# Attention in a one-core block kernel: high probabilities times the whole 129-column value row in one product for three of four query tiles, the low part added by VectorE

## The chip, the core and the metric

The kernel is written for one core of a Trainium2 chip. A core has TensorE (matrix products, with its own weight loads), VectorE, ScalarE and GpSimd, each with an instruction queue of its own that runs in order, and SyncE, which issues transfers. They share SBUF; products land in PSUM, eight banks of 512 fp32 columns. The metric is the device time of one execution, in microseconds, the median of several runs.

## What is computed

The input is `x`, 4 sequences of 1024 rows and 256 features. The reference adds to it, in turn, a linear recurrent block, a sparse feed-forward block, multi-head attention, and the feed-forward block again, each behind a layer norm. The change concerns attention:

```python
q = (x @ Wq.T).reshape(b, t, N_HEADS, HEAD_DIM)          # 8 heads of 64
kv_latent = x @ Wkv_down.T                               # 64 wide
k = (kv_latent @ Wk_up.T).reshape(b, t, N_HEADS, HEAD_DIM)
v = (kv_latent @ Wv_up.T).reshape(b, t, N_HEADS, HEAD_DIM)
scores = jnp.einsum('bqhd,bkhd->bhqk', q, k) * scale
attn = jax.nn.softmax(scores, axis=-1)
out = jnp.einsum('bhqk,bkhd->bqhd', attn, v)
return out.reshape(b, t, N_HEADS * HEAD_DIM) @ Wo.T
```

The kernel folds the up-projections into the query and output weights, so that all heads share the 64-wide latent as key and as value. To hold fp32 accuracy with fp16 products it splits the probabilities and the latent values into a high and a low fp16 part.

## The kernel before, in words

**Stages.** Recurrent block, first feed-forward block (the top-k rounds on VectorE), attention from about 500 to 1150 us, second feed-forward block. The order of work on each engine is written out by hand; engines meet through semaphores only.

**Items.** Attention is a loop over 64 items `W`: 4 batches, 8 heads, 2 chunks of 512 queries. In an item the key tile `kt` runs from 0 to 7 (128 keys each). TensorE issues, for each `kt`: `scores(W, kt)` (L2021 and L2023, two 512-column products), then `max_scores(W + 2, kt)` (L2009, one 512-column product on strided queries, used to find a row maximum two items ahead), then, at `kt` 3, 4, 6 and 7, one query tile `j` of `weighted(W - 1, j)`, and at some places "slot work": query and key projections, turns and the output projection of neighbouring batches (L1929 to L1967). Batch 0 has hardly any slot work.

**The other engines.** ScalarE takes the exponential of each score tile (L1154) and copies it to fp16 as the high part (L1162); one probability tile buffer `pr` serves all items, `pr_hi` and `pr_lo` are double. The low part, probability minus high part, is subtracted by GpSimd for key tiles 1, 2, 3, 5, 6, 7 (L830) and by VectorE for 0 and 4 (L1628). VectorE also reduces each `max_scores` product (L1602) in the order of tiles; three PSUM banks serve these, so `max_scores` number n waits for reduce n - 3. At the end of an item VectorE does `largest` (L1610) and then `normalise(W - 1)` (L1619 reciprocal, L1621 multiply by it, written to `o_sb`). In some items it adds the output projection to `x` (L1591) and takes layer-norm statistics (L1284, L1293).

**The product that is changed.** `lat` holds for each key a row of 1 + 64 + 64 fp16 numbers: a one, the high part of the latent value and its low part. For each query tile `j` and key tile, `weighted` issues three products into a 65-column strip of bank 5: high probabilities times [one, high value] (L2038, 65 columns), high probabilities times low value into the same columns 1 to 64 (L2039, 64 columns), low probabilities times [one, high value] (L2040, 65 columns). Column 0 becomes the sum of the probabilities. Ahead of query tile 0 of an item it waits for the latent values, for `a_O` (the previous item was normalised), and for the last low parts of VectorE and GpSimd. The last item has a function of its own, `weighted_last`, which writes to four banks and is not changed.

`out_turn` (L1960) transposes `o_sb` for the output projection of a batch and waits on `a_O` for all items of that batch, the last of which is normalised at the end of the first item of the next batch.

Of the kernel before, what the change touches and what calls it, by code (L numbers as in the profile page):

```python
# [9 lines left out]
ALU = mybir.AluOpType  # L10
# [7 lines left out]
CH = 512  # L18
NCH = ROWS // CH
TPC = CH // P  # L20
# [4 lines left out]
HD = 64  # L25
# [22 lines left out]
def hybrid_block_kernel(nc, x_in, W_in, b_in, params_log, W_mid, b_mid, w1_w, w1_b, w2_w, w2_b,  # L48
# [4 lines left out]
    with ctx:  # L53
# [3 lines left out]
        def sem(name):  # L57
            return ctx.enter_context(nc.semaphore(name))
# [49 lines left out]
        def carve(shape, dt=F32, parts=P):  # L108
            n = 1
            for s in shape:  # L110
                n *= s
            words = n if dt == F32 else (n + 1) // 2
            a = arena[0:parts, room[0]:room[0] + words]
            room[0] += words
            assert room[0] <= ARENA, room[0]
            if dt != F32:
                a = a.bitcast(dt)
            if len(shape) == 2:
                a = a.rearrange("p (a b) -> p a b", a=shape[0])
            if len(shape) == 3:  # L120
                a = a.rearrange("p (a b c) -> p a b c", a=shape[0], b=shape[1])
            return a
# [66 lines left out]
        pr_hi = [carve([TIME // P, CH], F16) for _ in range(2)]  # L189
        pr_lo = [carve([TIME // P, CH], F16) for _ in range(2)]  # L190
# [8 lines left out]
        lat = [carve([TIME // P, 1 + 2 * HD], F16) for _ in range(2)]  # L199
        mx = [carve([TPC]) for _ in range(2)]  # L200
        mx_half = [carve([TPC, 2]) for _ in range(2)]
        mx_row = [carve([TPC], F16) for _ in range(2)]
        rden = carve([TPC])
        o_sb = [xcT[:, :].rearrange("p (t d) -> p t d", t=TIME // P), carve([TIME // P, NH * HD])]
        staged = [o_sb[1].rearrange("p t d -> p (t d)")[:, i * 2 * CH // 2:(i + 1) * 2 * CH // 2].bitcast(F16)
                  .rearrange("p (h t) -> p h t", h=2) for i in range(2 * GROUPS)]
# [22 lines left out]
        psum = ctx.enter_context(nc.psum_tensor("banks", [P, 8, 512], F32))  # L229
        ps = [psum[:, i, :] for i in range(8)]  # L230
# [109 lines left out]
        a_lP = sem("a_exp_low_pool")  # L340
        a_ops = sem("a_out_psum")
        a_O = sem("a_out")
        a_ft = sem("a_oT_psum")
        a_fe = sem("a_oT")
        a_fm = sem("a_final_psum")
# [11 lines left out]
        KT = TIME // P  # L357
        MX = TPC
        L_STEPS = 10
        ALL = BATCH * ITEMS  # L360
# [61 lines left out]
        def low_done(W, kt):  # L422

            if W == ALL - 1:
                return ((W * len(LOW_DVE) + LAST_DVE.index(kt)) if kt in LAST_DVE else
                        (W * len(LOW_POOL) + LAST_POOL.index(kt))) + 1
            if kt in LOW_DVE:
                return W * len(LOW_DVE) + LOW_DVE.index(kt) + 1
            return W * len(LOW_POOL) + LOW_POOL.index(kt) + 1
# [15 lines left out]
        def place(W):  # L445

            B, w = W // ITEMS, W % ITEMS
            hh, c = w // 2, w % 2
            return B, hh, c, hh % Q_RING
# [24 lines left out]
        def wait_from(engine, sem_, value):  # L474

            if value > 0:
                engine.wait_ge(sem_, value)
# [759 lines left out]
        def _(dve):  # L1237
# [374 lines left out]
            def normalise(W):  # L1612

                B, hh, c, slot = place(W)
                o = ps[5][:, 0:TPC * (HD + 1)].rearrange("p (t d) -> p t d", t=TPC)
                if W == ALL - 1:
                    o = psum[:, 0:TPC, 0:HD + 1]
                dve.wait_ge(a_ops, W + 1)
                nc.vector.reciprocal(rden, o[:, :, 0]).then_inc(a_O, 1)  # L1619
                dve.wait_ge(a_O, W * 2 + 1)  # L1620
                nc.vector.tensor_tensor(o_sb[B % 2][:, c * TPC:c * TPC + TPC, hh * HD:hh * HD + HD],  # L1621
                                        o[:, :, 1:1 + HD],
                                        rden.unsqueeze(2).to_broadcast([P, TPC, HD]), ALU.mult).then_inc(a_O, 1)
# [20 lines left out]
            for W in range(ALL):  # L1644
                B, w = W // ITEMS, W % ITEMS
                for kt in range(KT):
                    if W + 2 < ALL:
                        largest_of(W + 2, kt)
                    if kt in (LAST_DVE if W == ALL - 1 else LOW_DVE):
                        low(W, kt)  # L1650
                    if kt == 5 and w in STATS_AT and AHEAD <= B + 1 < BATCH:
                        chunk = 2 * B + 2 + STATS_AT[w]
                        dve.wait_ge(f_x, chunk * TPC + TPC + CREDIT["f_x"])
                        stats_of("ffn", chunk)
                    if kt in (3, 7):
                        what, n, part = beside(W, kt // 7)
                        bank = BESIDE[kt // 7]
                        if what == "query":
                            query_low(n, part, bank)
                        if what == "out_final":  # L1660
                            final(n, bank)
                        if what == "keys":
                            keys_low(n, part, bank)
                if W + 2 < ALL:
                    largest(W + 2)
                if W:
                    normalise(W - 1)
            final((BATCH - 1) * FINALS - 1, 4)
            normalise(ALL - 1)
            for j in range(FINALS):  # L1670
                final((BATCH - 1) * FINALS + j, 6 + j % 2)
# [20 lines left out]
        def _(pe):  # L1692
            mm = nc.tensor.matmul
# [105 lines left out]
            def bank_for(n):  # L1799

                if n >= 2:
                    pe.wait_ge(s_ev0, n - 1)
                return ps[4 + n % 2]

            for k in range(KB2):
                o = bank_for(k)
                nc.tensor.transpose(o[:, 0:P], lin_n[:, k, :], ident[:, :]).then_inc(s_pe0, 1)
            for k in range(KB2):
                o = bank_for(2 + k)
                nc.tensor.transpose(o[:, 0:HD], wd_n[:, k * P:k * P + P], ident[0:HD, 0:HD]).then_inc(s_pe0, 1)  # L1810
            for a in range(NH // 2):
                o = bank_for(4 + a)
                for k in range(KB2):
                    last = nc.tensor.transpose(o[:, k * P:k * P + P], wo_n[:, k, a * P:a * P + P], ident[:, :])
                last.then_inc(s_pe0, 1)
            lru_u(1, 1, (0, 1))
            for a in range(NH // 2):
                o = bank_for(8 + a)
                pe.wait_ge(s_ev0, 5 + a)
                for r in (0, HD):  # L1820
                    last = mm(o[r:r + HD, 0:D], wv_n[r:r + HD, a, :], woT[r:r + HD, a, :], start=True, stop=True)
                last.then_inc(s_pe0, 1)
            for k in range(KB2):
                for odd in range(2):
                    o = bank_for(12 + 2 * k + odd)
                    for a in range(NH // 2):
                        rows = slice(HD * odd, HD * odd + HD)
                        last = mm(o[:, a * HD:a * HD + HD], wq_n[rows, a, k * P:k * P + P], wk_n[rows, a, :],
                                  start=True, stop=True)
# [196 lines left out]
            def weighted(W, j):  # L2026


                B, c = W // ITEMS, W % 2
                if j == 0:  # L2030
                    pe.wait_ge(a_l, B * 2 + 2)
                    wait_from(pe, a_O, W * 2)
                    pe.wait_ge(a_lD, low_done(W, LOW_DVE[-1]))
                    pe.wait_ge(a_lP, low_done(W, LOW_POOL[-1]))
                o = ps[5][:, j * (HD + 1):(j + 1) * (HD + 1)]
                js = slice(j * P, j * P + P)
                for kt in range(KT):
                    mm(o, pr_hi[c][:, kt, js], lat[B % 2][:, kt, 0:1 + HD], start=kt == 0, stop=False)  # L2038
                    mm(o[:, 1:1 + HD], pr_hi[c][:, kt, js], lat[B % 2][:, kt, 1 + HD:], start=False, stop=False)  # L2039
                    last = mm(o, pr_lo[c][:, kt, js], lat[B % 2][:, kt, 0:1 + HD], start=False, stop=kt == KT - 1)  # L2040
                if j == TPC - 1:
                    last.then_inc(a_ops, 1)

# [70 lines left out]
            for W in range(ALL):  # L2114
                for kt in range(KT):
                    scores(W, kt)
                    if W + 2 < ALL:
                        max_scores(W + 2, kt)
                    if kt in WEIGHTED_AT and W:
                        weighted(W - 1, WEIGHTED_AT[kt])  # L2120
                    if kt < 2:
                        slot_work(W, 0, kt)
                    if kt in (2, 5):
                        slot_work(W, 1, kt // 5)
# [45 lines left out]
```

## Time and profile before

| | |
|---|---|
| median of 3 runs | 1370.94 us (1370.88 to 1372.45) |
| profiled execution | 1372.7 us, its span 1371.0 us |
| TensorE products | 1221.7 us busy, 89% |
| VectorE | 1146.8 us, 84% |
| ScalarE | 1052.5 us, 77% |
| GpSimd | 960.3 us, 70% |
| L2038, L2039, L2040 | 2016 products each, 193, 195 and 192 ns shown |

The span is the time from the first to the last instruction of one profiled execution. "Busy" counts an instruction from its start to its shown end; neighbouring products overlap on TensorE, so its pace is read from the distances between starts. In rows of the timeline the columns are start in us, length in us, engine, line, operation, output and input by name, shape, how many merged into the row, and in brackets how long the engine had been idle and for whom it waited.

### The profile page before, as it was taken

How to read it: one execution, taken by the hardware profiler on the slowest of the kernel's cores; microseconds unless marked ns; L12 is line 12 of the kernel's file. 1: busy time of each engine (PE TensorE's matmuls, PEld its weight loads, DVE VectorE, ACT ScalarE, POOL GpSimd, SP SyncE). 2: the span in 40 equal slices, each digit the busy share in tenths (PEclk: the TensorE clock that was granted, in tenths of full speed). 3: DMA queues.
4: the chain of work that ended last, by engine and by line, in shares of the span. 5: the costliest groups of instructions: out<-in, count | busy, mean ns of one | idle time of the engine just before them, and what ended most of it. 6: DMA issues, size and time to landing. Idle time of an engine off the chain costs nothing.

```text
span 1371.0 us, 30692 instructions
## 1 busy us (share of the span) xinstructions
PE 1221.7 (89%) x10214; PEld 748.0 (55%) x10214; DVE 1146.8 (84%) x3145; ACT 1052.5 (77%) x2346; POOL 960.3 (70%) x1095
## 2 busy tenths in 40 slices
PE   4999999866888889999999999999999999777776
PEld 2455554434545446665666666676666666344443
DVE  7999998599998878888777788877877854799998
ACT  3432333787899859999989989999999986787776
POOL 4457644478787767777776778777777773488887
PEclk9999999998999989999999999999999999799998
DMA  6200000000002100000000000000000000000000
GB/s 173 79 1 1 1 0 0 1 1 1 24 32 78 39 1 25 25 25 25 25 14 13 2 2 2 2 2 2 2 2 2 2 2 1 1 32 17 31 16 32
DMA packets 35529, 25.32 MB, mean 18 GB/s; under 512 B 16358, under 2 KB 32044, under 8 KB 35372
## 3 DMA queue, kind: packets, MB, share of 16 engines
q1 hardware_dynamic: 35372, 23.36, 6.0%
q8 instruction: 82, 1.34, 0.4%
q14 instruction: 75, 0.61, 0.1%
HBM read 14.89 MB, written 8.39 MB: 17 GB/s over the span
## 4 chain that ended last, share of the span: by engine, by line
PE 44%; ACT 13%; issue 11%; DVE 9%; POOL 4%; DVEq 0%; ACTq 0%; POOLq 0%
PE banks L2021 7%; PE banks L2023 6%; PE banks L2009 6%; PE banks L1967 4%; DVE arena L1526 4%; PE banks L2038 4%; PE banks L2039 4%; PE banks L2040 3%; ACT arena L1154 3%; DVE arena L1521 3%; ACT arena L1162 2%; PE banks L1943 2%; PE banks L2080 2%; ACT arena L1016 1%; DVE arena L1602 1%
## 5 line engine op out<-in xcount | busy, mean ns | idle before, releaser
L830 POOL TENSOR_TENSOR arena<-arena 128x512 f16<-128x512 f32 x383 | 437.6, 1162 | 151.0 <-ACT arena L1162 147.0
L1154 ACT ACTIVATE arena<-banks 128x512 f32<-128x512 f32 x512 | 303.0, 599 | 45.4 <-PE banks L2023 40.9
L1602 DVE TENSOR_REDUCE arena<-banks 128x1 f32<-128x512 f32 x512 | 325.5, 679 | 7.8 <-PE banks L2009 5.5
L1162 ACT ACTIVATE arena<-arena 128x512 f16<-128x512 f32 x512 | 316.1, 632 | 0.0
L2038 PE MATMUL banks<-arena 128*128 128x65 f16 x2016 | 211.3, 193 | 0.9
L1521 DVE MAX8 arena<-arena 128x8 f32<-128x256 f32 x512 | 190.1, 413 | 25.7 <-issue 13.9
L2039 PE MATMUL banks<-arena 128*128 128x64 f16 x2016 | 211.4, 195 | 0.0
L2040 PE MATMUL banks<-arena 128*128 128x65 f16 x2016 | 210.5, 192 | 0.0
L1628 DVE TENSOR_TENSOR arena<-arena 128x512 f16<-128x512 f32 x129 | 106.8, 828 | 123.4 <-ACT arena L1162 123.3
L1526 DVE MATCH_REPLACE8 arena<-arena 128x256 f32<-128x256 f32 x512 | 205.8, 409 | 1.7 <-issue 1.2
L2038 PEld LDWEIGHTS banks<-arena 128*128 128x128 f16 x2016 | 187.9, 96 | 31.8 <-issue 9.9
L2039 PEld LDWEIGHTS banks<-arena 128*128 128x128 f16 x2016 | 187.3, 97 | 27.1
L2021 PE MATMUL banks<-arena 128*128 128x512 f16 x512 | 194.1, 379 | 8.4 <-ACT arena L1154 6.7
L2009 PE MATMUL banks<-arena 128*128 128x512 f16 x512 | 195.1, 383 | 4.3 <-DVE arena L1602 4.0
L2023 PE MATMUL banks<-arena 128*128 128x512 f16 x512 | 193.8, 378 | 0.0
L2040 PEld LDWEIGHTS banks<-arena 128*128 128x128 f16 x2016 | 187.3, 99 | 0.0
L1890 PE MATMUL banks<-fW,arena 128*128 128x256 f32 x256 | 81.9, 448 | 31.8 <-ACT arena L1042 31.8
L2009 PEld LDWEIGHTS banks<-arena 128*128 128x128 f16 x512 | 57.9, 113 | 74.9 <-DVE arena L1602 16.2
L1877 PE MATMUL banks<-fW,arena 128*128 128x256 f32 x256 | 77.2, 431 | 0.0
L2021 PEld LDWEIGHTS banks<-arena 128*128 128x128 f16 x512 | 50.3, 98 | 48.9 <-ACT arena L1154 31.3
L1890 PEld LDWEIGHTS banks<-fW,arena 128*128 128x128 f32 x256 | 47.5, 206 | 51.9 <-ACT arena L1042 47.5
L1869 PE MATMUL banks<-lin,xcT 128*128 128x512 f32 x128 | 70.0, 629 | 0.4 <-ACT xcT L1046 0.4
(230 smaller groups left out, 2543.1 us busy)
## 6 DMA issues: line engine op xcount, KB each, us to landing
arena<-q_store SPq DMA_DIRECT2D x48, 128.0 KB, 2.7
x<-in_L_attn_a_x SPq DMA_DIRECT2D x8, 512.0 KB, 3.9
q_store<-arena SPq DMA_DIRECT2D x32, 128.0 KB, 1.8
out<-x SPq DMA_DIRECT2D x7, 512.0 KB, 2.9
arena<-arena SPq DMA_DIRECT2D x64, 1.0 KB, 1.9
arena<-in_L_attn_a_W_in SPq DMA_DIRECT2D x1, 768.0 KB, 5.6
arena<-in_L_attn_a_W_mid SPq DMA_DIRECT2D x1, 512.0 KB, 7.0
arena<-in_L_attn_a_w_w SPq DMA_DIRECT2D x2, 256.0 KB, 7.5
```

The lines of the kernel that those rows point to most:

```text
L830: nc.gpsimd.tensor_tensor(pr_lo[c][:, kt, :], pr[:, kt, :], pr_hi[c][:, kt, :], ALU.subtract).then_inc(a_lP, 1)
L1154: nc.scalar.activation(pr[:, kt, :], ps[6 + kt % 2][:, :], ACT.Exp, scale=SM_SCALE).then_inc(a_P, 1)
L1162: nc.scalar.activation(pr_hi[c][:, kt, :], pr[:, kt, :], ACT.Copy).then_inc(a_hi, 1)
L1521: nc.vector.max(m8[p][:, i, r, :], src).then_inc(f_k[i], 1)
L1526: nc.vector.match_replace(wk[p][:, i, r % 2, :], m8[p][:, i, r, :], src, TAKEN).then_inc(f_k[i], 1)
L1602: nc.vector.tensor_reduce(mx_half[c][:, i // 2, i % 2:i % 2 + 1], ps[n % MAX_BANKS][:, :], X, ALU.max).then_inc(a_mx, 1)
L2009: mm(ps[n % MAX_BANKS][:, :], every[:, j, :], kA[B % 2][:, half * CH:half * CH + CH], start=True, stop=True).then_inc(a_mps, 1)
L2021: mm(o[:, :], kA[B % 2][:, kt * P:kt * P + P], qA[:, slot, c * CH:c * CH + CH], start=True, stop=False)
L2023: mm(o[:, :], kB[B % 2][:, kt * P:kt * P + P], qB[:, slot, c * CH:c * CH + CH], start=False, stop=True).then_inc(a_sps, 1)
L2038: mm(o, pr_hi[c][:, kt, js], lat[B % 2][:, kt, 0:1 + HD], start=kt == 0, stop=False)
L2039: mm(o[:, 1:1 + HD], pr_hi[c][:, kt, js], lat[B % 2][:, kt, 1 + HD:], start=False, stop=False)
L2040: last = mm(o, pr_lo[c][:, kt, js], lat[B % 2][:, kt, 0:1 + HD], start=False, stop=kt == KT - 1)
```

## The change

For query tiles 0 to 2 the two products with the high probabilities become one of 129 columns, into a strip of 129 columns of bank 5; the third product, with the low probabilities, still goes to the first 65 of them. The strip of tile 3 starts at column 387 and only has 125 columns left, so that tile keeps its three products. `normalise` now takes the strips 129 apart. For every item but the last it first copies the low strips of three tiles (3 x 64 columns) to a new SBUF tile `o_low`, takes the reciprocal, adds `o_low` onto columns 1 to 64 of the three tiles in PSUM, and then multiplies as before. The semaphore `a_O_low` orders copy, add and multiply on VectorE.

```diff
@@ -201,6 +201,7 @@
+        o_low = carve([TPC - 1, HD])
@@ -340,6 +341,7 @@
+        a_O_low = sem("a_out_low_part")
@@ -1612,11 +1614,19 @@
             def normalise(W):
 
                 B, hh, c, slot = place(W)
-                o = ps[5][:, 0:TPC * (HD + 1)].rearrange("p (t d) -> p t d", t=TPC)
+                o = psum[:, :, :].rearrange("p b c -> p (b c)")[:, 5 * CH:5 * CH + TPC * (1 + 2 * HD)]
+                o = o.rearrange("p (t d) -> p t d", t=TPC)
+                dve.wait_ge(a_ops, W + 1)
                 if W == ALL - 1:
                     o = psum[:, 0:TPC, 0:HD + 1]
-                dve.wait_ge(a_ops, W + 1)
+                else:
+                    nc.vector.tensor_copy(o_low, o[:, 0:TPC - 1, 1 + HD:]).then_inc(a_O_low, 1)
                 nc.vector.reciprocal(rden, o[:, :, 0]).then_inc(a_O, 1)
+                if W < ALL - 1:
+                    dve.wait_ge(a_O_low, W * 2 + 1)
+                    nc.vector.tensor_tensor(o[:, 0:TPC - 1, 1:1 + HD], o[:, 0:TPC - 1, 1:1 + HD], o_low,
+                                            ALU.add).then_inc(a_O_low, 1)
+                    dve.wait_ge(a_O_low, W * 2 + 2)
                 dve.wait_ge(a_O, W * 2 + 1)
@@ -2032,12 +2042,16 @@
-                o = ps[5][:, j * (HD + 1):(j + 1) * (HD + 1)]
+                o = ps[5][:, j * (1 + 2 * HD):min(CH, (j + 1) * (1 + 2 * HD))]
                 js = slice(j * P, j * P + P)
                 for kt in range(KT):
-                    mm(o, pr_hi[c][:, kt, js], lat[B % 2][:, kt, 0:1 + HD], start=kt == 0, stop=False)
-                    mm(o[:, 1:1 + HD], pr_hi[c][:, kt, js], lat[B % 2][:, kt, 1 + HD:], start=False, stop=False)
-                    last = mm(o, pr_lo[c][:, kt, js], lat[B % 2][:, kt, 0:1 + HD], start=False, stop=kt == KT - 1)
+                    if j < TPC - 1:
+                        mm(o, pr_hi[c][:, kt, js], lat[B % 2][:, kt, :], start=kt == 0, stop=False)
+                    else:
+                        mm(o[:, 0:1 + HD], pr_hi[c][:, kt, js], lat[B % 2][:, kt, 0:1 + HD], start=kt == 0, stop=False)
+                        mm(o[:, 1:1 + HD], pr_hi[c][:, kt, js], lat[B % 2][:, kt, 1 + HD:], start=False, stop=False)
+                    last = mm(o[:, 0:1 + HD], pr_lo[c][:, kt, js], lat[B % 2][:, kt, 0:1 + HD], start=False,
+                              stop=kt == KT - 1)
```

## Rows read from the trace of the kernel before

**Rows 1.** The page: busy us, share of the span, instructions of each engine.
```profile
PE 1221.7 (89%) x10214; PEld 748.0 (55%) x10214; DVE 1146.8 (84%) x3145; ACT 1052.5 (77%) x2346; POOL 960.3 (70%) x1095
```

**Rows 2.** Reciprocals (L1619) in three stretches: ns min/median/max, first and last start.
```profile
L1619 DVE RECIPROCAL arena<-banks x11: 171/172/175, 514.1 to 599.5; 128x4 f32<-128x4 f32 x11
...
L1619 DVE RECIPROCAL arena<-banks x44: 163/172/183, 633.8 to 1083.6; 128x4 f32<-128x4 f32 x44
...
L1619 DVE RECIPROCAL arena<-banks x3: 171/172/172, 1083.6 to 1100.7; 128x4 f32<-128x4 f32 x3
```

**Rows 3.** Windows: length, busy us of PE, PEld, DVE, ACT, POOL, clock, DMA share, GB/s.
```profile
514.00:599.50 85.50, 84.67 (x1202) 52.59 (x1201) 70.88 (x132) 82.99 (x172) 67.95 (x61) 1.00 0.09 25
633.00:1083.60 450.60, 441.42 (x5557) 294.49 (x5556) 355.59 (x693) 413.54 (x824) 338.44 (x328) 1.00 0.03 6
```

**Rows 4.** Chain of work by line, 514 to 599.5 us and 640 to 1083 us.
```profile
by line: PE banks L2021 22.5%; PE banks L2023 20.2%; PE banks L2009 20.2%; PE banks L2038 13.1%; PE banks L2039 11.7%; PE banks L2040 11.4%; issue 1.0%
...
by line: PE banks L2021 12.9%; PE banks L2023 12.6%; PE banks L2009 12.2%; PE banks L1967 8.2%; PE banks L2039 7.0%; PE banks L2040 6.8%; ACT arena L1154 6.8%; PE banks L2038 6.7%; PE banks L1943 5.6%; issue 5.0%; ACT arena L1162 4.5%; DVE 
```

**Rows 5.** Timeline of TensorE, batch 0: one burst of weighted and its neighbours.
```profile
558.39 0.38 PE L2009 MATMUL banks<-arena 128*128 128x512 f16 x1
558.82 0.19 PE L2038 MATMUL banks<-arena 128*128 128x65 f16 x1
...
559.56 0.38 PE L2021 MATMUL banks<-arena 128*128 128x512 f16 x1
...
559.99 0.38 PE L2009 MATMUL banks<-arena 128*128 128x512 f16 x1
```

**Rows 6.** Timeline of GpSimd and ScalarE, batch 0.
```profile
555.29 3.38 POOL L830 TENSOR_TENSOR arena<-arena 128x512 f16<-128x512 f32 x3 [1.01 <-ACT arena L1162]
...
561.63 0.60 ACT L1154 ACTIVATE arena<-banks 128x512 f32<-128x512 f32 x1 [0.25 <-PE banks L2023]
...
563.83 3.38 POOL L830 TENSOR_TENSOR arena<-arena 128x512 f16<-128x512 f32 x3 [1.01 <-ACT arena L1162]
```

**Rows 7.** Timeline of TensorE: 128-column fp16 products at 958.92 us.
```profile
958.92 0.28 PE L1951 MATMUL banks<-ident,arena 128*128 128x128 f16 x2
959.03 0.38 PE L2021 MATMUL banks<-arena 128*128 128x512 f16 x1
```

**Rows 8.** Timeline of VectorE, batch 0, from one item's normalise on.
```profile
556.77 0.16 DVE L1610 TENSOR_REDUCE arena<-arena 128x4 f32<-128x8 f32 x1
556.84 0.17 DVE L1619 RECIPROCAL arena<-banks 128x4 f32<-128x4 f32 x1
557.05 0.42 DVE L1621 TENSOR_TENSOR xcT<-banks,arena 128x256 f32<-128x256 f32 x1
557.39 0.68 DVE L1602 TENSOR_REDUCE arena<-banks 128x1 f32<-128x512 f32 x1
558.30 0.93 DVE L1628 TENSOR_TENSOR arena<-arena 128x512 f16<-128x512 f32 x1 [0.24 <-ACT arena L1162]
559.15 2.47 DVE L1602 TENSOR_REDUCE arena<-banks 128x1 f32<-128x512 f32 x4
562.78 0.69 DVE L1628 TENSOR_TENSOR arena<-arena 128x512 f16<-128x512 f32 x1 [1.15 <-ACT arena L1162]
563.39 0.68 DVE L1602 TENSOR_REDUCE arena<-banks 128x1 f32<-128x512 f32 x1
```

**Rows 9.** Timeline of VectorE and TensorE at 676 us.
```profile
675.89 0.68 DVE L1602 TENSOR_REDUCE arena<-banks 128x1 f32<-128x512 f32 x1
...
676.63 0.41 PE L2009 MATMUL banks<-arena 128*128 128x512 f16 x1
```

**Rows 10.** Waits, 640 to 1083 us: us in total, times, longest.
```profile
DVE arena L1628 <- ACT arena L1162: 83.9, 76, 1.8
```

**Rows 11.** Who waited for L1621, and two such places in TensorE's timeline.
```profile
  PE banks L1960: 3.5, 3
...
812.30 0.63 PE L1960 MATMUL banks<-ident,arena 128*128 128x128 f32 x4 [1.67 <-DVE arena L1621]
812.76 0.38 PE L2021 MATMUL banks<-arena 128*128 128x512 f16 x1
...
1132.46 0.74 PE L1960 MATMUL banks<-ident,arena 128*128 128x128 f32 x5 [1.48 <-DVE arena L1621]
```

## The prediction

> **What bounds the kernel now.** I read the share of busy time first [rows 1]: TensorE 89% and VectorE 84% of the span, so neither can be dismissed, and the average says nothing about the stage that is changed. The change lies wholly in the attention stage, where 64 items run one after another; I next read their pace and the windows. Items of batch 0 follow each other at 8.54 us (eleven from 514.1 to 599.5), the three from 1083.6 to 1100.7 too; those between, with query, turn and output work beside them, at 10.5 us (44 from 633.8 to 1083.6) [rows 2]. In both stretches TensorE's modelled busy time is 98 to 99%, ScalarE's 92 to 97%, VectorE's 79 to 83% [rows 3]. The chain of work points to TensorE [rows 4]: the three product lines of `weighted` (L2038 to L2040) hold 36% of it in batch 0 and 20.5% from 640 to 1083 us, where other engines stand between.
>
> In batch 0 that share misleads, and I follow one period. `weighted` starts at 558.82 [rows 5] because GpSimd's last subtraction is done (three from 555.29, 3.38 us, so at 558.67 [rows 6]). After it come two bursts and two pairs of score products, then exponential 5 on ScalarE (561.63, 0.25 us idle for TensorE), then GpSimd's next three subtractions from 563.83 [rows 6], done at 567.21, and `weighted` again at about 567.35. This loop, 8.53 us, holds only two of the four bursts.
>
> **The products.** In 63 items (the last has code of its own) three of four query tiles lose one 64-column product for each of 8 key tiles: 63 x 3 x 8 = 1512 products and their weight loads go, and as many products grow from 65 to 129 columns. A burst of 24 products runs from 558.82 to 559.56 [rows 5]: 0.74 us, or 92 ns for each group of three; products overlap, so I count starts and not the 190 ns that one is shown to take. The trace has no 129-column product. Two fp16 products of 128 columns start at 958.92 and the next work at 959.03 [rows 7]: 55 ns each; one more column, by the 0.215 us of 512 columns (two between 559.56 and 559.99, rows left out between them), makes about 56. With one low product at 29 to 33 ns (a third of 92 is 31) a group is 85 to 89 ns. I take 85.5, since a long product leaves the next weight load time: 6.5 ns saved a group, 0.05 us a burst, 0.155 us an item. Bounds: 3 and 7 ns.
>
> The Trainium skill (TensorE: Matmul & The Clock Gate, section Back-to-back issue gap) speaks against the change: a stream of weight loads with 128-column matmuls sustains some 81 ns for each, not 56. This trace does not agree so far, with 55 ns [rows 7], though in a run of only two. By that figure a group would take about 110 ns instead of 92.
>
> **What VectorE gets.** `normalise` gains a copy of 3 x 64 values out of PSUM and an add of that size into PSUM, with two waits for the engine's own results. The trace has neither. The multiply of 256 values is shown as 0.42 us and gives way after 0.34 (557.05 to 557.39); reduces of 512 follow each other every 0.60 (four in 2.47 us, the last shown as 0.68) [rows 8]. That is 1.0 ns a value, so 192 values occupy 0.27 us and are shown as 0.35. An operation that needs the one before starts 0.04 us after its shown end (556.84 + 0.17, then 557.05). So: copy at 0, reciprocal at 0.27, add at 0.39, multiply at 0.78; before, the multiply came 0.21 after the reciprocal. Added: 0.57 us an item. Bounds: 0.45 if the copy runs twice as fast, 0.75 if the write into PSUM and the waits cost 0.1 each more.
>
> Queued behind it on VectorE are the largest-of reduce 0 (L1602), the subtraction of key tile 0 (L1628) and reduces 1 to 4. TensorE's `max_scores` i+3 must have reduce i, and stands in its queue ahead of `weighted`. TensorE's own wait on `a_O` comes 2 us later and stays covered, except at output turns (below).
>
> *The 17 plain items.* VectorE idles 0.24 us before the subtraction at 558.30. Reduce 1 ends at 559.15 + 0.69 = 559.84 and max_scores 4 starts at 559.99 [rows 5, 8]; where it truly waits, the gap is 0.05 (675.89 + 0.68 to 676.63 [rows 9]), so 0.10 is slack. New loop: subtraction 4 (562.78), reduces 5 to 7, `normalise`, reduce 0, subtraction 0, reduce 1, max_scores 4, a burst, exponential 5, subtraction 4. Its length: 8.53 + 0.57 - 0.24 - 0.10 - 0.05 = 8.71. Against that, the subtraction at 558.30 holds the engine 0.85 us, beside GpSimd's that runs until 558.67 [rows 6], while the one at 562.78 holds it 0.61 [rows 8]. Started a third of a microsecond later it hardly meets that work: up to 0.24 less, 8.47. The old loop would give 8.53 - 0.10 = 8.43. I take 8.56, nearer to the short ends because both effects are seen in rows: +0.03 x 17 = +0.5 us. Ends 8.43 and 8.71: -1.7 to +3.1.
>
> *The 43 others.* There VectorE's subtractions wait for ScalarE 76 times, 1.10 us in the mean [rows 10], nearly every one of two an item; the added 0.57 vanishes in the first of them. The gain is what the chain holds: 20.5% of 443 us is 91, three quarters of it in changed bursts, x 6.5/92 = -4.8 us. At 3 ns it is -2.2; if every burst counted, 43 x 0.155 = -6.7.
>
> *Where `normalise` is itself waited for.* TensorE's turn of the output (L1960) waits for the multiply three times, 3.5 us in all [rows 11], because VectorE was occupied by statistics; each costs the full 0.57: +1.7 us. Two of them are at 812.30 and, behind the last item, 1132.46. At 675.89 a reduce behind `normalise` is awaited without slack [rows 9]: +0.5. For a few items with little slack I add 0.2, an estimate.
>
> **Sum.** +0.5 - 4.8 + 1.7 + 0.7 = -1.9 us. The profiled execution has a span of 1371.0 and a time of 1372.7; the difference goes to the median of the runs, 1370.94: 1369.0.
>
> **The rivals.**
> 1. *TensorE's gain goes through almost whole.* For: TensorE is busy 98% in the window of the 43. -1.7 from the plain items, -6.7, +2.4: 1364.9. Against: ScalarE has 92% there, so some of the gain must end in a wait for it.
> 2. *VectorE takes over the period of the plain items* (slower). Place: the wait of max_scores 4 for reduce 1. It decides once the addition exceeds 0.39 us while the subtraction keeps its 0.85. At 0.75 the period is 8.89: +6.1 for 17 items, output turns +2.3, the other places +1.0, products -4.8: +4.6, 1375.5. For: VectorE's order is fixed and only 1.4 us of such an item is idle [rows 8]. Against: the shrinking overlap with GpSimd.
> 3. *The wide product does not run at its columns' pace.* Priced half way between the fp16 pace of 55 ns and that of fp32 products of 128 columns (four in 0.46 us, 812.30 to 812.76 [rows 11], 115 ns): 85, a group 115, 23 ns more, 0.55 us an item. 43 x 0.55 x two thirds on the chain is +15.8, two bursts of 0.18 in 17 items +6.3, VectorE +2.4: 1395.4. Rows 7 speak against it.
>
> The skill's page named above gives about the product pace of rival 3.
>
> **How the numbers follow.** The forecast, 1367 to 1371.5, has 45%, rival 1 25%, rival 2 25%, rival 3 5%. The range of 8 in 10 is 1364.0 to 1376.0: it takes in rivals 1 and 2 and leaves rival 3 out. A measurement of this kernel can tell 0.2%, 2.7 us, from no change. Faster than 1368.2 are rival 1 and a third of the forecast's case, 0.39; slower than 1373.7 are 18 in 25 of rival 2 and rival 3, 0.23; within, 0.38.
>
> **What would show it.** Starts inside a changed burst: 56 and 29 ns alternating, the burst 0.685 us; if the second is 33, the gain halves. Reciprocals of batch 0 8.56 us apart: 8.43 means that VectorE never binds, 8.7 or more that it does, with a gap on TensorE ahead of L2009. The multiply 0.78 us after the copy's start. The three waits for the output turn longer by 0.57 each. I should be wrong most easily on the chain's share in the 43 items, since a faster TensorE meets ScalarE sooner.

## The result, and the profile of the changed kernel

| | kernel before | changed kernel |
|---|---|---|
| median | 1371.24 us (20 runs, 1368.09 to 1374.29) | 1374.11 us (20 runs, 1371.87 to 1378.33) |
| ratio | | 1.002, 95% interval 1.0012 to 1.0029 |
| profiled execution | 1372.7 us, span 1371.0 | 1374.12 us, span 1372.4 |

The change costs 2.9 us, 0.2%, where 1.9 us less had been forecast. The page shows both parts of the change: TensorE has 1512 products fewer and 9 us less to do, VectorE 31 us more [rows 1].

```profile
PE 1212.9 (88%) x8702; PEld 739.0 (54%) x8702; DVE 1177.6 (86%) x3271; ACT 1052.7 (77%) x2346; POOL 958.8 (70%) x1095
```

In the windows that answer to [rows 3], batch 0 and the items after it, TensorE is busy 97% where it was 98 to 99, and VectorE 84 to 85% where it was 79 to 83.

```profile
514.00:599.80 85.80, 83.64 (x960) 51.70 (x959) 72.99 (x150) 83.27 (x170) 67.53 (x61) 1.00 0.09 25
635.10:1085.10 450.00, 437.16 (x4519) 290.08 (x4520) 378.96 (x775) 411.86 (x820) 335.78 (x326) 1.00 0.03 6
```

The timeline of TensorE in a plain item, which answers to [rows 5], shows the new burst: from 557.85 to 558.55, 0.70 us where it was 0.74. A product of 129 columns gives way after 0.05 to 0.06 us, the low product behind it after 0.03. Ahead of the burst `max_scores` 3 starts at 557.48, and it has been waiting for VectorE's reduce.

```profile
557.48 0.41 PE L2019 MATMUL banks<-arena 128*128 128x512 f16 x1 [0.17 <-DVE arena L1604]
557.85 0.22 PE L2049 MATMUL banks<-arena 128*128 128x129 f16 x1
557.90 0.19 PE L2053 MATMUL banks<-arena 128*128 128x65 f16 x1
557.93 0.22 PE L2049 MATMUL banks<-arena 128*128 128x129 f16 x1
557.99 0.19 PE L2053 MATMUL banks<-arena 128*128 128x65 f16 x1
...
558.55 0.38 PE L2031 MATMUL banks<-arena 128*128 128x512 f16 x1
```

In this item the burst starts 0.37 us behind the product that had waited. That is not typical: from 514 to 618 us the distance is 0.24 to 0.25 us in 11 of 13 items and 0.30 in one. The item after it shows the common case, with GpSimd's three subtractions ahead, which end at 566.16:

```profile
562.78 3.38 POOL L832 TENSOR_TENSOR arena<-arena 128x512 f16<-128x512 f32 x3 [1.19 <-ACT arena L1164]
...
566.20 0.41 PE L2019 MATMUL banks<-arena 128*128 128x512 f16 x1 [0.17 <-DVE arena L1604]
566.44 0.22 PE L2049 MATMUL banks<-arena 128*128 128x129 f16 x1
```

VectorE's timeline of the first of these two items answers to [rows 8]. From the copy at 555.62 to the multiply at 556.40 are 0.78 us. The subtraction at 557.34 has no idle time in front of it any more, and it holds the engine 0.60 us and not 0.85.

```profile
555.54 0.16 DVE L1612 TENSOR_REDUCE arena<-arena 128x4 f32<-128x8 f32 x1
555.62 0.35 DVE L1623 COPY arena<-banks 128x192 f32<-128x192 f32 x1
555.88 0.17 DVE L1624 RECIPROCAL arena<-banks 128x4 f32<-128x4 f32 x1
556.00 0.37 DVE L1627 TENSOR_TENSOR banks<-banks,arena 128x192 f32<-128x192 f32 x1
556.40 0.42 DVE L1631 TENSOR_TENSOR xcT<-banks,arena 128x256 f32<-128x256 f32 x1
556.74 0.68 DVE L1604 TENSOR_REDUCE arena<-banks 128x1 f32<-128x512 f32 x1
557.34 0.68 DVE L1638 TENSOR_TENSOR arena<-arena 128x512 f16<-128x512 f32 x1
557.94 2.48 DVE L1604 TENSOR_REDUCE arena<-banks 128x1 f32<-128x512 f32 x4
561.73 0.69 DVE L1638 TENSOR_TENSOR arena<-arena 128x512 f16<-128x512 f32 x1 [1.31 <-ACT arena L1164]
```

**Where the time went.** Whole spans are a poor measure here: the work ahead of attention, which the change does not touch, took 0.5 to 4.1 us less in the profiles of the experiments than in that of the kernel before. So I take the starts of ScalarE's exponential of key tile 0 in each item. The distance to the next one is that item's time, and the tail runs from item 63's to the last turn of the output (L1960). The plain items are 2 to 16, 59 and 60. The table gives the differences in us against the profile of before; its last three columns are the two runs that do one part alone (below) and their sum:

| | before | changed | VectorE's part alone | products alone | the two added |
|---|---|---|---|---|---|
| items 0 and 1 | 16.81 | -0.11 | +0.01 | -0.09 | -0.08 |
| 17 plain items | 145.36 | +1.01 | +1.95 | -1.10 | +0.85 |
| 40 later items | 415.04 | -2.92 | +0.07 | -2.93 | -2.86 |
| item 17 (output turn) | 10.76 | +0.93 | +0.94 | -0.03 | +0.91 |
| item 20 | 9.48 | +0.51 | +0.58 | -0.07 | +0.51 |
| item 33 (output turn) | 12.79 | +2.04 | +0.58 | +0.12 | +0.70 |
| item 49 | 11.32 | +0.27 | +0.18 | +0.01 | +0.19 |
| tail (output turns) | 28.12 | +1.74 | +2.10 | -0.06 | +2.04 |
| sum | | +3.47 | +6.41 | -4.15 | +2.26 |

The products bring 4.2 us, most of it in the later items, where VectorE's extra work costs nothing. Of what the changed kernel loses, 1.0 us lies in the plain items and 5.5 in four items and the tail, places where VectorE is late with layer-norm statistics. The two parts added explain the changed kernel to within 0.3 us in each line but that of item 33, where 1.3 us are unexplained by them.

**The half clock.** The windows of the changed kernel show what is in item 33 and in the tail. The column behind the five engines is the granted clock.

```profile
810.00:812.80 2.80, 0.45 (x4) 0.22 (x3) 2.54 (x12) 1.59 (x3) 2.38 (x4) 1.00 0.00 0
812.80:816.00 3.20, 3.20 (x24) 2.31 (x23) 3.20 (x6) 1.49 (x3) 0.32 (x1) 0.50 0.01 3
1133.60:1137.20 3.60, 3.60 (x13) 2.85 (x11) 0.00 (x0) 1.19 (x2) 0.58 (x2) 0.53 0.00 0
```

The kernel before kept the full clock behind the same two waits:

```profile
812.20:816.00 3.80, 3.70 (x61) 2.78 (x61) 3.77 (x7) 2.47 (x6) 1.89 (x2) 1.00 0.00 0
1132.40:1136.00 3.60, 3.20 (x20) 2.77 (x21) 0.13 (x1) 1.08 (x2) 1.02 (x2) 1.00 0.00 0
```

TensorE's timeline of the changed kernel, beside [rows 11]: it had waited 2.35 us and 2.06 us for `normalise`, where it had been 1.67 and 1.48. Behind the first wait its 512-column products start 0.42 to 0.43 us apart (813.33, 813.75, 814.18) and not 0.215: 1.2 GHz in place of 2.4.

```profile
812.61 0.93 PE L1970 MATMUL banks<-ident,arena 128*128 128x128 f32 x4 [2.35 <-DVE arena L1631]
813.33 0.63 PE L2031 MATMUL banks<-arena 128*128 128x512 f16 x1
813.75 0.64 PE L2033 MATMUL banks<-arena 128*128 128x512 f16 x1
814.18 0.63 PE L2019 MATMUL banks<-arena 128*128 128x512 f16 x1
...
1133.21 1.54 PE L1970 MATMUL banks<-ident,arena 128*128 128x128 f32 x8 [2.06 <-DVE arena L1631]
1134.67 3.14 PE L1977 MATMUL banks<-voB,arena 128*128 128x256 f32 x8
1137.65 0.60 PE L1970 MATMUL banks<-ident,arena 128*128 128x128 f32 x4
```

### The profile page after: what moved, and what is told of

It reads as the page before. It is cut to its first block, busy times and chain, and to the rows that moved or that the text cites. A ratio compares the mean times of both kernels' runs of the same rounds, so it can differ in the third digit from the quotient of the medians.

```text
span 1372.4 us, 27857 instructions
## 1 busy us (share of the span) xinstructions
PE 1212.9 (88%) x8702; PEld 739.0 (54%) x8702; DVE 1177.6 (86%) x3271; ACT 1052.7 (77%) x2346; POOL 958.8 (70%) x1095
## 4 chain that ended last, share of the span: by engine, by line
PE 33%; ACT 19%; issue 12%; DVE 10%; POOL 6%; DVEq 0%; DMA 0%; SPq 0%; POOLq 0%; ACTq 0%
ACT arena L1156 6%; ACT arena L1164 5%; PE banks L2031 4%; PE banks L2033 4%; PE banks L2019 4%; PE banks L1977 4%; DVE arena L1528 4%; POOL arena L832 3%; PE banks L2049 3%; DVE arena L1523 3%; PE banks L2053 2%; PE banks L1953 2%; PE banks L2094 2%; ACT arena L1018 1%; DVE arena L1604 1%
## 5 line engine op out<-in xcount | busy, mean ns | idle before, releaser
L2053 PE MATMUL banks<-arena 128*128 128x65 f16 x2016 | 205.7, 193 | 0.0
L2053 PEld LDWEIGHTS banks<-arena 128*128 128x128 f16 x2016 | 181.4, 98 | 19.7 <-issue 0.3
L1638 DVE TENSOR_TENSOR arena<-arena 128x512 f16<-128x512 f32 x129 | 103.0, 798 | 94.7 <-ACT arena L1164 93.0
L2049 PE MATMUL banks<-arena 128*128 128x129 f16 x1512 | 158.1, 221 | 0.1
L2049 PEld LDWEIGHTS banks<-arena 128*128 128x128 f16 x1512 | 136.7, 97 | 19.6 <-issue 2.2
L1900 PE MATMUL banks<-fW,arena 128*128 128x256 f32 x256 | 80.3, 441 | 32.0 <-ACT arena L1044 32.0
L2019 PEld LDWEIGHTS banks<-arena 128*128 128x128 f16 x512 | 57.9, 113 | 83.7 <-DVE arena L1604 27.1
L2031 PEld LDWEIGHTS banks<-arena 128*128 128x128 f16 x512 | 50.2, 98 | 49.9 <-ACT arena L1156 29.6
L1887 PE MATMUL banks<-fW,arena 128*128 128x256 f32 x256 | 72.8, 411 | 0.0
L768 POOL TENSOR_TENSOR arena<-arena 128x256 f32<-128x256 f32 x63 | 45.8, 727 | 32.0 <-ACT arena L1039 27.8
L1025 ACT ACTIVATE arena<-arena 128x256 f32<-128x256 f32 x128 | 57.9, 503 | 12.7 <-DVE arena L1528 12.7
## 6 DMA issues: line engine op xcount, KB each, us to landing
x<-in_L_attn_a_x SPq DMA_DIRECT2D x8, 512.0 KB, 3.8
out<-x SPq DMA_DIRECT2D x7, 512.0 KB, 2.9
arena<-in_L_attn_a_W_mid SPq DMA_DIRECT2D x1, 512.0 KB, 7.5
```

The lines of the kernel that those rows point to most:

```text
L1900: last = mm(ps[6][:, 0:D], sxT[p][:, k, :], fW[:, k, :], start=k == 0, stop=k == KB2 - 1)
L2019: mm(ps[n % MAX_BANKS][:, :], every[:, j, :], kA[B % 2][:, half * CH:half * CH + CH], start=True, stop=True).then_inc(a_mps, 1)
L2031: mm(o[:, :], kA[B % 2][:, kt * P:kt * P + P], qA[:, slot, c * CH:c * CH + CH], start=True, stop=False)
L2049: mm(o, pr_hi[c][:, kt, js], lat[B % 2][:, kt, :], start=kt == 0, stop=False)
L2053: last = mm(o[:, 0:1 + HD], pr_lo[c][:, kt, js], lat[B % 2][:, kt, 0:1 + HD], start=False, stop=kt == KT - 1)
```

## The experiments

My theory was: TensorE's saving is real and partly hidden; VectorE's 0.57 us costs in plain items and at the output turns; and two longer waits of TensorE lower its clock. The rivals: the wide product saves nothing, VectorE's work is hidden, or the extra time in item 33 and the tail is VectorE's delay itself.

### One part alone

VectorE's part alone:

```diff
-                        mm(o, pr_hi[c][:, kt, js], lat[B % 2][:, kt, :], start=kt == 0, stop=False)
+                        mm(o[:, 0:1 + HD], pr_hi[c][:, kt, js], lat[B % 2][:, kt, 0:1 + HD], start=kt == 0, stop=False)
+                        mm(o[:, 1 + HD:], pr_hi[c][:, kt, js], lat[B % 2][:, kt, 1 + HD:], start=False, stop=False)
```

> VectorE's part alone: the strips lie 129 apart and VectorE copies and adds as in the change, but tiles 0 to 2 keep two short products for the high probabilities (65 and 64 columns). Theory (VectorE's 0.57 us costs by itself, at output turns with a half-clock stretch behind them; TensorE's saving gives a part back): items of batch 0 at 8.68 us, the time 6 to 9 us over the kernel before. Rival (VectorE's work is hidden, the loss is the wide product's): within 1 us of before.

Measured: 1377.69 us against 1370.94 of the kernel before on the same chip, ratio 1.0048 (1.0035 to 1.0061), +6.7 us. Plain items take 8.66 us (598.1 less 511.5, by 10).

```profile
L1624 DVE RECIPROCAL arena<-banks x11: 170/172/173, 511.5 to 598.1; 128x4 f32<-128x4 f32 x11
```

The products alone. The low part of the values is left out for three of four query tiles, so this kernel's results are not complete (lines between the cut ones are left out here):

```diff
-                    nc.vector.tensor_copy(o_low, o[:, 0:TPC - 1, 1 + HD:]).then_inc(a_O_low, 1)
...
-                    nc.vector.tensor_tensor(o[:, 0:TPC - 1, 1:1 + HD], o[:, 0:TPC - 1, 1:1 + HD], o_low,
-                                            ALU.add).then_inc(a_O_low, 1)
```

> TensorE's part alone: wide products as in the change, but no copy and no add in normalise, so the low part of the values is left out for three of four query tiles. Theory: items of batch 0 at 8.45 us, the 43 items behind them a few hundredths to 0.2 us shorter each, in all 4 us below the kernel before. Rival (the wide product saves nothing that counts): within 1 us of before.

Measured: 1367.40 us against 1370.94, ratio 0.9972 (0.996 to 0.9984), -3.5 us; plain items 8.48 us. Both rivals fall. The products do pay, VectorE's part is dearer, and the two results, +6.7 and -3.5, give +3.2, about the 2.9 of the whole.

```profile
L1622 DVE RECIPROCAL arena<-banks x11: 171/172/175, 512.8 to 597.6; 128x4 f32<-128x4 f32 x11
```

### TensorE kept busy in its two long waits

TensorE gets eight products of 512 columns, whose results nobody reads, ahead of the output turn of item 33 and of the first one behind item 63 (there into bank 7):

```diff
                 if what == "out_turn" and half == 0:
+                    if W == 2 * ITEMS + 1:
+                        kept_busy(bank, 8)
...
+                    if j == 0:
+                        kept_busy(7, 8)
                     out_turn(J, j % 2)
```

> The changed kernel, with eight products of 512 columns of no use (1.7 us) put into TensorE's two long waits, ahead of the output turn in item 33 and of the one behind item 63. Theory (the waits, 2.7 and 2.2 us, let the granted clock fall to half for the next 3.5 us): granted clock 1.00 behind both waits, item 33 shorter by 1.4 us, the tail by 1.2, the time 2.6 us below the changed kernel. Rival (the extra 2 us there are VectorE's delay itself): same as the changed kernel or a little longer.

The 2.7 and 2.2 us of this expectation run from the start of the product before the wait to the start of the one behind it; the idle time in the rows above is 2.35 and 2.06. Measured: 1370.06 us against 1370.94, ratio 0.9992 (0.9982 to 1.0003). Item 33 is +0.62 above before, not +2.04; the tail +0.44, not +1.74; every other line of the table stays within 0.25 us of the changed kernel's. So the half clock cost 1.4 and 1.3 us. VectorE's delay at the two places is then about 0.6 and 0.4 us. Windows behind the waits:

```profile
811.00:815.00 4.00, 3.47 (x32) 2.04 (x31) 3.74 (x14) 2.03 (x5) 1.85 (x3) 1.00 0.01 2
1133.00:1137.00 4.00, 3.66 (x20) 3.21 (x20) 0.42 (x1) 1.35 (x3) 0.11 (x1) 1.00 0.01 4
```

The same products in the kernel before:

> The same useless products in the kernel before, whose waits are 2.0 and 1.7 us and where the profiled execution kept the full clock. Theory: no change, within 0.5 us, unless other executions of the kernel before lose the clock there too. Rival: any gain would mean that they do.

Measured: 1370.78 us against 1370.94, ratio 0.9996 (0.9988 to 1.0005). The kernel before gains nothing from them, so its waits do not cost it the clock. The rival "it is VectorE's delay itself" falls.

To see whether the half clock was an accident of one execution, the changed kernel unaltered:

> The changed kernel once more, unaltered, beside the three below. Theory (the half-clock stretches belong to the change in most executions): item 33 and the tail again 2.0 and 1.7 us above the kernel before, the time 2.5 to 3.5 us above it. Rival (one execution's accident): item 33 only 0.6 above, no stretch at half clock.

Measured: 1373.24 us against 1371.42, ratio 1.0016 (1.0007 to 1.0024). Item 33 +2.05, tail +1.83, and the granted clock behind the waits is 0.54 both times:

```profile
812.80:816.00 3.20, 3.20 (x24) 2.21 (x24) 3.20 (x6) 1.65 (x3) 0.47 (x1) 0.54 0.01 3
1133.60:1137.20 3.60, 3.51 (x13) 2.69 (x12) 0.00 (x0) 1.19 (x2) 0.58 (x2) 0.54 0.00 0
```

VectorE's part alone shows the other side: it lost the clock in the tail (+2.10) but not in item 33 (+0.58), though TensorE had waited 2.24 us there. So the length of the wait does not settle it alone. The timed runs give only the total, so how often it is lost in each place stays open.

```profile
813.25 0.63 PE L1970 MATMUL banks<-ident,arena 128*128 128x128 f32 x4 [2.24 <-DVE arena L1631]
...
813.30:817.00 3.70, 3.70 (x61) 2.70 (x61) 3.67 (x7) 2.52 (x6) 1.16 (x2) 1.00 0.01 2
```

### VectorE's addition doubled

The second copy and add work on the low strips, which nobody reads afterwards (the first wait's new number and the last wait are left out):

```diff
+                    nc.vector.tensor_copy(o_low2, o[:, 0:TPC - 1, 1 + HD:]).then_inc(a_O_low, 1)
+                    dve.wait_ge(a_O_low, W * 4 + 3)
+                    nc.vector.tensor_tensor(o[:, 0:TPC - 1, 1 + HD:], o[:, 0:TPC - 1, 1 + HD:], o_low2,
+                                            ALU.add).then_inc(a_O_low, 1)
```

> The changed kernel with a second copy and a second add of the same shape in normalise, on the low strips that nobody reads afterwards: VectorE gets another 0.65 to 0.8 us an item. Theory (the 0.57 of the change hides in VectorE's wait of 1.1 us in the 40 later items, and a plain item has nothing left to hide the next): plain items 8.60 plus the whole addition, about 9.3, +11 us for 17; the 40 later items gain 0 to 0.3 us each; output turns +0.7 each; together 15 to 25 us above the changed kernel.

Measured: 1394.47 us against 1371.42, ratio 1.0174 (1.0157 to 1.019), 21 us above the unaltered changed kernel timed beside it. A second copy and add occupy 0.79 us (559.43 to 560.22), and plain items take 9.39 us (596.5 less 512.0, by 9): 8.60 plus all of the 0.79. In the 40 later items it costs 2.6 us in all, 0.07 each. So the plain items had some cover for VectorE before the change and have none behind it, and in the later items the cover reaches more than twice as far.

```profile
559.43 0.36 DVE L1631 COPY arena<-banks 128x192 f32<-128x192 f32 x1
559.82 0.37 DVE L1633 TENSOR_TENSOR banks<-banks,arena 128x192 f32<-128x192 f32 x1
560.22 0.42 DVE L1637 TENSOR_TENSOR xcT<-banks,arena 128x256 f32<-128x256 f32 x1
...
L1625 DVE RECIPROCAL arena<-banks x10: 173/173/174, 512.0 to 596.5; 128x4 f32<-128x4 f32 x10
```

### Room for the output turns

Two moves: in the second item of a batch TensorE turns the output later, and behind the last item VectorE normalises ahead of its layer-norm statistics.

```diff
-                if what == "out_turn" and half == 0:
+                if what == "out_turn" and half == (1 if W % ITEMS == 1 else 0):
...
-            final((BATCH - 1) * FINALS - 1, 4)
+            final((BATCH - 1) * FINALS - 1, 4, stats=False)
+            dve.wait_ge(a_O, (ALL - 1) * 2)
             normalise(ALL - 1)
+            dve.wait_ge(a_fx, (BATCH - 1) * FINALS)
+            stats_of("out", (BATCH - 1) * FINALS // TPC - 1)
```

> The kernel before with two moves that make room ahead of the output turns: in the second item of a batch TensorE issues the turn at key tile 5, not 2, and behind the last item VectorE normalises it ahead of the layer-norm statistics. Theory (TensorE waits there only because VectorE is at statistics): items 17 and 33 shorter by 0.4 and 1.7 us, the tail by 0.6; 2.7 us below the kernel before.

> The changed kernel with the same two moves. Theory (three output turns and two half-clock stretches behind them cost the change about 3.5 us, plain items 1 us): item 33 shorter by 3.5 us and the tail by 2.5, no stretch at half clock, plain items still 8.60; some 6.5 us below the changed kernel, and 0.5 to 1 us below the kernel before with the two moves. Rival (VectorE's 0.57 us is paid somewhere else when it is not paid there): the two kernels with the moves differ by 2 us or more in favour of the old products.

Measured: 1369.52 (ratio 0.999, 0.9979 to 1.0) and 1370.60 (ratio 1.0, 0.9989 to 1.001), against 1371.34. The tail did as expected, -0.58 and -0.65 against before, that is 2.4 below the changed kernel. Item 33 did not: -0.48 where -1.7 was expected, and +0.83 with the change where -1.5 was. The waits of the kernel before with the moves (engine, line, waited for: us in total, times, longest) show why. TensorE no longer waits for `normalise` there but 1.7 us for the reduce of a `max_scores` bank, which is late for the same reason:

```profile
PEld banks L2012 <- DVE arena L1602: 2.5, 2, 2.2
PE banks L2012 <- DVE arena L1602: 1.7, 1, 1.7
```

VectorE is full in those items, and moving the one who asks first only changes who waits. The moved turn also costs time in the items behind, 18 and 34: +0.35 and +0.57 us in the kernel before, which is more than the 0.26 and 0.48 gained in items 17 and 33. With item 33, this is why both kernels missed their expectation. With both moves there is no half clock, though the changed kernel's TensorE waits 2.53 us ahead of a `max_scores` at 810.93 (granted clock 1.00 from 806 to 815 us), and the changed products are 0.6 us behind the old ones by the table, 1.1 us by the medians. I had expected them 0.5 to 1 us ahead. That was a miss too, though the rival's 2 us is not reached either.

### normalise behind the first reduce

A third move: in VectorE's queue `normalise` stands behind reduce 0 of the next item.

```diff
                         largest_of(W + 2, kt)
+                    if kt == 0 and W > 1:
+                        normalise(W - 2)
...
-                if W:
-                    normalise(W - 1)
+            normalise(ALL - 2)
```

With the two moves above:

> The kernel before with the two moves and a third: normalise stands behind reduce 0 of the next item in VectorE's queue. Theory: plain items stay at 8.53, which GpSimd's subtraction sets; within 0.5 us of the kernel with two moves.

> The changed kernel with all three moves. Theory (in plain items max_scores 3 waits for reduce 0, which stands behind normalise): plain items fall from 8.60 to 8.48, the pace of the products alone, 2 us below the changed kernel with two moves. Rival (VectorE as a whole is too slow, and the delay moves on to reduce 1): plain items 8.55 to 8.60, no gain.

Measured: 1370.64 (ratio 0.9993, 0.9982 to 1.0004) and 1368.75 (ratio 0.9983, 0.9973 to 0.9993), against 1371.34. Plain items of the changed kernel fall to 8.48 us, the pace of the products alone; those of the kernel before stay at 8.54. The rival (the delay moves on to reduce 1) falls. In the table's terms the two kernels stand at -0.6 and -1.9 us. This version beats both: 2.6 us below the kernel before, the only complete kernel of the study whose interval lies below 1. Its gain over the kernel before with the same three moves is 1.9 us by the medians.

```profile
L1624 DVE RECIPROCAL arena<-banks x11: 173/173/174, 510.9 to 595.7; 128x4 f32<-128x4 f32 x11
```

Without the two moves:

> The changed kernel with only the third move, normalise behind reduce 0 of the next item. Theory: plain items 8.48 (-2.1 us in 17), the output turns wait 0.6 us longer for it, the half-clock stretches stay: 0.5 to 2 us below the changed kernel.

Measured, for the third move alone: 1374.25 against 1371.42, ratio 1.0024 (1.0014 to 1.0034). Plain items are right, -1.13 in the table's line against +1.01. But the later `normalise` costs it at item 33 (+2.77), item 49 (+0.91) and the tail (+2.14), and the gain is gone: +3.2 in sum, where the changed kernel has +3.5. By the median it is no better than the changed kernel; the expectation was missed.

The third move with the useless products of above:

> The third move and the eight useless products in each of the two long waits. Theory: plain items 8.48 and full clock everywhere; 4 to 5 us below the changed kernel, 1 to 3 us below the kernel before.

Measured: 1372.91 against 1371.42, ratio 1.0006 (0.9996 to 1.0015), where 1 to 3 us below the kernel before had been expected. Item 33 (+1.38) and the tail (+0.44) keep the clock. Item 17, which has no useless products, is +2.69 where the run without them had +1.16: the clock was lost there, around waits of only 1.05 and 1.57 us (a window and two rows of TensorE's timeline, then the window behind the wait and the two rows of the run without the useless products). The run without them had the same two waits and kept the full clock. What made the difference stays open.

```profile
645.00:649.00 4.00, 4.00 (x36) 2.77 (x35) 2.93 (x5) 1.65 (x4) 1.46 (x2) 0.66 0.03 4
...
641.90 0.41 PE L2022 MATMUL banks<-arena 128*128 128x512 f16 x1 [1.05 <-DVE arena L1604]
...
644.52 1.09 PE L1971 MATMUL banks<-ident,xcT 128*128 128x128 f32 x4 [1.57 <-DVE xcT L1631]
...
644.20:648.00 3.80, 3.80 (x46) 2.77 (x47) 3.70 (x5) 2.32 (x5) 2.05 (x3) 1.00 0.03 5
...
641.56 0.41 PE L2020 MATMUL banks<-arena 128*128 128x512 f16 x1 [1.05 <-DVE arena L1604]
...
644.18 0.63 PE L1971 MATMUL banks<-ident,xcT 128*128 128x128 f32 x4 [1.57 <-DVE xcT L1631]
```

## Why the prediction was wrong, by its own steps

- **VectorE's price, 0.57 us: right.** Copy to multiply took 0.78 us as worked out; the bounds were not needed.
- **The group of products, 85.5 ns: near.** It is 87.5 ns (0.70 us for 8 groups). 55 ns for a long product came from a run of two; in the bursts it is between 56 and 62. The old groups took 92 ns, so the saving is 4.5 ns and not 6.5. Over 1512 long products the 81 ns for a 128-column product in a stream, by the Trainium skill (TensorE: Matmul & The Clock Gate, section Back-to-back issue gap), do not hold here: rival 3 is out.
- **Plain items, 8.56 us: 8.60, +1.0 where +0.5 was said.** (The second profile of the changed kernel has +0.8.) The products alone reach 8.48, where 8.43 was said. Two effects were seen rightly: the subtraction for key tile 0 fell from 0.85 to 0.60 us, and the idle 0.24 us in front of it is gone. The loop is closed at another link than I named, by reduce 0 and not by reduce 1. TensorE's `max_scores` 3 waits for reduce 0, which stands right behind `normalise` and now ends together with GpSimd's last subtraction. In the kernel before, and with the products alone, `max_scores` 3 is out of the way by then and the burst starts 0.15 us behind GpSimd (558.67 to 558.82 [rows 5, 6]). Now it has to go first, and the burst starts 0.28 us behind GpSimd (566.16 to 566.44). That is the 0.12 us by which 8.60 exceeds 8.48, and with `normalise` moved behind reduce 0 it is gone. Most of it stands in the rows that I had: by [rows 5, 8] and the 0.05 of [rows 9] reduce 0 would end at 558.64, `max_scores` 3 start at 558.69 and the burst 0.22 later, 0.09 behind its old place. I tested only the wait for reduce 1.
- **The later items, -4.8: -2.9.** The cover for VectorE was read rightly (+0.07 alone). The gain was too large twice: 4.5 ns a group in place of 6.5 makes -3.3 of it, and the products alone bring no more than -2.9. That the chain's share overstated the gain by the last 0.4 is what is left over, not something a run shows.
- **Where `normalise` is waited for, +1.7 and +0.7: this is the step that failed.** "Each costs the full 0.57" took a longer wait to cost nothing but its own length, and the sum had no term for the clock. As a delay it was right: items 17, 20, 33 and 49 and the tail, at full clock, come to 0.93 + 0.51 + 0.62 + 0.27 + 0.44 = 2.8, where 2.4 was said. But two of the waits grew from 1.67 and 1.48 us to 2.35 and 2.06, and behind them TensorE ran at half clock for more than 3 us: 1.4 and 1.3 us more. I looked at the granted clock in no window around the waits that the change would lengthen. With the clock kept the change is no measurable change (0.9992, 0.9982 to 1.0003), which is still short of the forecast: the -1.9 us needed the later items' -4.8 as well. The half clock is the larger error, 2.7 us, and the later items the second, 1.9.
- **The sum.** Terms in the order of the prediction: +1.0 (0.5), -2.9 (-4.8), +2.8 (2.4), half clock +2.7 (none), items 0 and 1 -0.1: +3.5 in the profile, +2.9 by the medians. Rival 2 gave the right side, and 1375.5, but that is luck: its plain items hold 1.0 us and not 6.1, and it has no half clock.

## What to carry to other kernels

Cheaper work on the busiest engine, paid for on the next one, has to be costed at the places where that next one is already late, not by its average idle time: here 40 of 64 items absorbed all of the 0.57 us, and four items and the tail carried most of the loss. When a change lengthens a wait of TensorE, look at the granted clock behind it, for the products after the wait may lose more than the wait grew (item 33: 1.4 us against 0.6). One execution is not enough for this, since equal waits kept the clock in one run and lost it in another. And when a step is added to an engine's queue, look at who is queued right behind it: moving the step one place down was worth 2 us in the plain items, all of their loss and more. By itself it gained nothing, because the places where `normalise` is waited for got later; only with the two other moves did it pay.

## What the runs showed of the hardware

- The granted clock stood at 0.50 to 0.54 of full behind waits of 2.35 and 2.06 us, in both profiles of the changed kernel, and at 1.00 behind 1.67 and 1.48 us in the kernel before. But it also stayed at 1.00 behind 2.24 us (VectorE's part alone) and 2.53 us (the changed kernel with two moves), and of two runs with the same waits of 1.05 and 1.57 us one kept it and one had 0.66 in a window of 4 us. No limit for the wait can be read from this; the clock came back some 3 to 4 us later. Useless products in the wait kept it at 1.00 both times.
- An fp16 subtraction of 512 values on VectorE held it 0.85 us when it started 0.37 us before the end of a subtraction of GpSimd (558.30 and 558.67), and 0.60 us when it started 0.12 before (557.34 and 557.46). A delay on VectorE thus paid back 0.25 us of itself. With VectorE's addition doubled, VectorE's subtraction started first, at 561.16, and kept its 0.60 us, while GpSimd's, started at 561.18, took 1.67 us where others of that run take 1.16: the one that started second was the longer one both times.
- A 129-column product with its own weight load starts the next one after 56 to 62 ns in most cases. The groups of three short ones that it partly replaces took 92 ns, some 4 to 5 ns above three of 29.
